# Graph attention and convolution on one core: products over 64 rows widened to 96 rows in the node stages

## The chip, the cores and the metric

The kernel runs on one core of one Trainium2 chip. The metric is the device time of one execution in microseconds (us). A core has TensorE (matrix products: weights are loaded, then columns are streamed through them), VectorE, ScalarE and GpSimd for element-wise work, and SyncE, which here only issues DMAs. The profile calls them PE (PEld for TensorE's weight loads), DVE, ACT, POOL and SP.

## The reference

6250 nodes with 160 features (64 scalars and 32 vectors of 3 components), 206250 edges sorted by their target. First a graph attention, then a graph convolution; both end in a residual and a layer norm over a node's features. What matters for the change are the products per node, cut from both layers:

```python
s_n, v_n = _equiv_layernorm(s, v, gamma_s, beta_s, gamma_v)      # per node
msg_s = (s_n @ Ws_src)[src] + (s_n @ Ws_dst)[dst]                # 64x64 each
msg_v = einsum('ncx,cd->ndx', v_n, Wv_src)[src] + einsum('ncx,cd->ndx', v_n, Wv_dst)[dst]
...                                                              # attention over edges
out = node + concatenate([agg_s @ Wps, einsum('ncx,cd->ndx', agg_v, Wpv)])
x = _layernorm(x + out)
# convolution
si_s, si_v = _irreps_linear(s_in, v_in, si_w0, si_w1)            # skip path, per node
h_s, h_v = _irreps_linear(s_in, v_in, lin1_w0, lin1_w1)          # gathered by the edges
...
x = _layernorm(x + s_skip + conv_out / 10.0)
```

## The kernel before, in words

The nodes lie in 49 blocks of 128 (nodes on partitions, features along the free dimension), the vectors with one component after the other, so that a block is 64 scalar columns and 96 vector columns. Everything is float32; a product appears in the trace as two passes (two weight loads and two MATMUL records), a transpose as one.

The kernel is a row of stages, each a block with its own instruction stream per engine and a barrier at its end:

1. attention_input: normalises the nodes and writes two tables, source and target, to memory.
2. attention_edges: gathers from them for 404 groups of 512 edges, computes logits and values.
3. segment_softmax, attention_aggregate: softmax over the edges of a node, sums into `agg`.
4. attention_output: divides by the softmax sum, projects (`wps`, `wpv`), adds to the nodes, layer norm, and projects again (`ts1`, `tv1`) into the table of the convolution and the skip path.
5. conv_edges, conv_output: the convolution over 452 steps, then the last products and the last layer norm.

The change lies in stages 1 and 4, from some 13 to 147 us and from 5236.5 to 5423 us of the span.

**attention_input.** Per block b, TensorE transposes the 64 scalar columns (L349) and the 96 vector columns (L350) into one bank of two; ScalarE moves them to SBUF with gamma and beta (L215, L217) into one buffer `feat` of four; TensorE multiplies: the 64 scalar rows with `ts0` (L356, 64 rows, 128 columns out) and the 96 vector rows with `tv0` (L358, 96 rows, 192 columns out) into one bank of four; VectorE copies the 320 columns to `out` (L337), and SyncE stores every half chunk. TensorE issues the transposes of block m ahead of the products of block m - 1. The nodes are normalised by VectorE in chunks of 3, 4 and six times 7 blocks (`EARLY0`); the eight steps of the next chunk's norm (L255 to L275) are spread between the copies of this chunk, and the last two steps (with L275 as the last) come after the copy of the last block but one. The transposes of a chunk wait for its last step. At b = 20 there is one more product (L362), over 64 rows. In the first 45 us GpSimd squares the edge vectors (L225 to L229) beside this.

**attention_output.** Two such pipelines run in one loop over m. The first ("u", block m): transposes L1132 and L1133, copy by ScalarE L1164 (96 partitions, 256 columns), products L1144 (`wps`, 64 rows, 64 columns out) and L1145 (`wpv`, 96 rows, 96 columns out), addition to the nodes by VectorE L1100. The second ("t", block m - 14, since its nodes must be normalised first, in chunks of 7): transposes L1138 and L1139, copy L1170, products L1152 (`ts1`, 64 rows, 128 columns out) and L1154 (`tv1`, 96 rows, 192 columns out), table copy by ScalarE L1178, skip addition by VectorE L1121. On TensorE the order in an iteration is L1132, L1133, L1138, L1139, L1144, L1145, L1152, L1154; the first 14 iterations have the u pair alone, the last 14 the t pair alone. All banks and feature buffers are double. VectorE also has the softmax division (L1057 to L1065, once per 7 blocks) and the norm (L1077 to L1092) in its stream.

In these transposes the scalars' one already takes 96 columns (`agg[:, b, 0:V3]`), of which the product reads 64 rows:

```python
pe.transpose(bt_u[b % 2][0:V3, 0:P], agg[:, b, 0:V3], w("ident"))
pe.matmul(bo_u[b % 2][:, 0:CS], feat_u[b % 2][0:CS, 0, :], w("wps"), start=True, stop=True)
```

`feat` is the stationary operand of each product (the profile's LDWEIGHTS, rows*columns "64*128" or "96*128"), the packed weights of `PACK` stream. `PACK` says for each weight how many rows it has; they all lie in one array of 128 partitions, filled on the host by `lay_pack`.

**conv_output** has products too (L1438, L1439, L1440), all over 128 rows, behind three transposes (L1432); it is not changed.

## Time and profile before

| | us |
|---|---|
| median of 3 runs (lowest to highest) | 7921.6 (7917.41 to 7922.39) |
| the profiled execution | 7914.6 |
| its span | 7912.8 |
| attention_input, to its last copy | 0 to 147.5 |
| attention_edges, softmax, aggregation | 147.5 to 5236 |
| attention_output, first transpose to last addition | 5236.6 to 5423.4 |
| conv_edges, conv_output | 5423 to 7912.8 |

The span is the time from the first to the last instruction of the profiled execution; its own time has what lies around that, 1.8 us. Starts in the rows below are us from the span's start. A row of the timeline has the start, the length, the engine, the line, the operation, what it writes and reads, the shape, and in brackets how long the engine had been idle and who released it; "x2" means that two records in a row were put together. The ends of MATMUL records are modelled, so distances between starts are safer than lengths. "issue" is idle time in which the engine waited for nothing that the profile shows. The clock is the one granted to TensorE as a share of 2.4 GHz.

### The profile page before, as it was taken

The page shows a single profiled execution, that of the slowest core. Times are in us where ns is not written, and L with a number is a line of the kernel's source. Part 1 is how long each engine was busy: PE and PEld are TensorE (multiplying, and loading weights), DVE is VectorE, ACT ScalarE, POOL GpSimd, SP SyncE. Part 2 cuts the span into 40 slices and gives each one's busy share as a digit, 9 for nine tenths or more (in the row PEclk, how much of TensorE's full clock was granted, in tenths as well). Part 3 has the DMA queues.
Part 4 walks back from the last instruction along what each step waited for, and adds up shares of the span by engine and source line. Part 5 has one row for each costly group of instructions (what it writes and reads, how often), then busy time and mean ns, then how long its engine had stood idle before and what let it go on. Part 6 is the DMA issues. An engine that isn't in the chain of part 4 may idle for free. (4 is left out here: it accounts for less than half of the span.)

```text
span 7912.8 us, 199441 instructions
## 1 busy us (share of the span) xinstructions
PE 7045.1 (89%) x48227; PEld 5905.9 (75%) x48227; DVE 7568.2 (96%) x18615; ACT 5259.2 (66%) x18286; POOL 5348.1 (68%) x5500
## 2 busy tenths in 40 slices
PE   6999999999999999999999859998888888888888
PEld 4888888888888888888888848875555555555556
DVE  4999999999999999999999889976999999999999
ACT  2666666666666666666666634435788788788786
POOL 2777777777777777777777436634777777777773
PEclk5999999999999999999999979977999999999999
DMA  3444444434434344343434337732333333333332
GB/s 105 107 109 109 106 107 106 107 106 106 107 105 107 106 107 106 106 108 105 107 106 107 89 128 260 257 117 69 94 93 91 90 91 90 91 91 90 91 91 59
DMA packets 815660, 856.41 MB, mean 108 GB/s; under 512 B 413920, under 2 KB 623200, under 8 KB 815072
## 3 DMA queue, kind: packets, MB, share of 16 engines
q0 software_dynamic: 241920, 413.20, 21.8%
q1 hardware_dynamic: 573088, 438.30, 18.1%
q10 hardware_dynamic: 576, 4.01, 0.1%
q8 instruction: 33, 0.54, 0.0%
q14 instruction: 43, 0.35, 0.0%
HBM read 706.51 MB, written 148.44 MB: 108 GB/s over the span
## 5 line engine op out<-in xcount | busy, mean ns | idle before, releaser
L1243 POOL DMA_INDIRECT agg<-tab_conv,ce_idx x1808 | 1708.7, 945 | 841.3 <-issue 621.8
L471 POOL DMA_INDIRECT ae_gdst<-tab_dst,ae_idx x1616 | 1683.9, 1042 | 528.0 <-issue 528.0
L468 POOL DMA_INDIRECT ae_gsrc<-tab_src,ae_idx x1616 | 1538.5, 952 | 674.4 <-issue 523.9
L1333 PE MATMUL psum<-ce_prod,ce_plain 128*128 128x384 f32 x3616 | 1539.7, 507 | 302.5 <-ACT ce_prod L1318 302.1
L1318 ACT ACTIVATE ce_prod<-ce_raw,ce_y 128x64 f32<-128x64 f32 x5424 | 1464.8, 333 | 0.0
L1316 ACT ACTIVATE ce_prod<-ce_raw,ce_y 128x160 f32<-128x160 f32 x1808 | 753.2, 417 | 488.8 <-DVE ce_raw L1264 488.8
L1335 PEld LDWEIGHTS psum<-ce_prod,ce_plain 128*128 128x128 f32 x3616 | 687.6, 190 | 479.6 <-issue 1.5
L713 ACT ACTIVATE ae_second_t<-psum 128x512 f32<-128x512 f32 x1212 | 732.2, 604 | 462.0 <-PE psum L623 456.1
L1333 PEld LDWEIGHTS psum<-ce_prod,ce_plain 128*128 128x128 f32 x3616 | 546.9, 191 | 449.5 <-DVE ce_plain L1294 276.2
L631 PE MATMUL psum<-pack_sb,ae_first_t 128*128 128x200 f32 x3232 | 850.1, 345 | 2.2 <-ACT ae_first_t L709 2.0
L641 PE MATMUL psum<-pack_sb,ae_second_t 128*128 128x96 f32 x3232 | 665.1, 288 | 129.1 <-ACT ae_second_t L713 126.7
L709 ACT ACTIVATE ae_first_t<-psum 128x512 f32<-128x512 f32 (+1 forms) x1212 | 692.0, 610 | 40.6 <-PE psum L614 40.6
L641 PEld LDWEIGHTS psum<-pack_sb,ae_second_t 128*128 128x128 f32 x3232 | 486.5, 190 | 241.6 <-issue 164.3
L614 PE MATMUL psum<-pack_sb,ae_first 128*128 128x128 f32 (+1 forms) x4848 | 662.9, 273 | 0.8 <-ACT ae_first_t L709 0.8
L719 ACT ACTIVATE ae_values<-psum 128x256 f32<-128x256 f32 x808 | 310.4, 384 | 523.8 <-PE psum L643 523.8
L1335 PE MATMUL psum<-ce_prod,ce_plain 128*128 128x96 f32 x3616 | 646.8, 261 | 0.0
L681 PE MATMUL psum<-pack_sb,ae_rbfy 64*128 64x224 f32 x3232 | 419.2, 374 | 255.0 <-DVE ae_first L540 231.1
L948 POOL TENSOR_TENSOR ag_exval<-ag_val,ag_wide 128x384 f32<-128x384 f32 x452 | 385.2, 852 | 380.9 <-ACT ag_exval L968 190.3
L643 PE MATMUL psum<-pack_sb,ae_second_t 128*128 128x96 f32 x3232 | 625.9, 275 | 0.0
L633 PE MATMUL psum<-pack_sb,ae_first_t 96*128 96x96 f32 x3232 | 625.8, 275 | 0.0
L642 PE MATMUL psum<-pack_sb,ae_second_t 128*128 128x96 f32 x3232 | 625.8, 275 | 0.0
L765 ACT ACTIVATE ae_second<-agg,ae_y_late 128x192 f32<-128x192 f32 x1616 | 598.2, 444 | 0.0
(216 smaller groups left out, 19066.1 us busy)
## 6 DMA issues: line engine op xcount, KB each, us to landing
ag_val<-h_dram SPq DMA_DIRECT2D x452, 320.0 KB, 4.0
h_dram<-ae_hout SPq DMA_DIRECT2D x404, 320.0 KB
agg<-in_query SPq DMA_DIRECT2D x452, 128.0 KB
ae_rin<-in_rin SPq DMA_DIRECT2D x404, 128.0 KB
agg<-tab_conv,ce_idx POOLq DMA_INDIRECT x1808
ae_gsrc<-tab_src,ae_idx POOLq DMA_INDIRECT x1616
ae_gdst<-tab_dst,ae_idx POOLq DMA_INDIRECT x1616
ce_idx<-in_eidx SPq DMA_DIRECT2D x452, 4.0 KB
```

What stands on the lines that cost most here:

```text
L468: pool.indirect_dma_start(gsrc[t.slot4][:, k, :], None, g["tab_src"], bass.IndirectOffsetOnAxis(ap=idx[t.slot4][:, k:k + 1], axis=0))\
L471: pool.indirect_dma_start(gdst[t.slot4][:, k, :], None, g["tab_dst"], bass.IndirectOffsetOnAxis(ap=idx[t.slot4][:, 4 + k:5 + k], axis=0))\
L614: ins = pe.transpose(b_t[b % 2][0:rows, P * k:P * k + P], first[t.slot][:, k, lo:lo + rows], w("ident"))
L631: pe.matmul(b_m[:, i, 0:200], first_t[0][:, e], w("m1_0"), start=True, stop=False)
L641: pe.matmul(b_h[:, i, 0:96], second_t[0][:, e], w("m2_0"), start=True, stop=False, skip_group_check=True)
L709: act.activation(first_t[b][0:rows, :], b_t[b % 2][0:rows, :], ACT.Copy).then_inc(kept, 1)
L713: act.activation(second_t[b][:, :], b_t[(b + 1) % 2][:, :], ACT.Copy).then_inc(kept2, 1)
L1243: pool.indirect_dma_start(node[t.slot8][:, k, :], None, g["tab_conv"], bass.IndirectOffsetOnAxis(ap=idx[t.slot8][:, k:k + 1], axis=0))\
L1316: act.activation(prod[t.slot][:, k, 0:160], raw[t.slot][:, k, 0:160], ACT.Identity, scale=y[t.slot8][:, k, 0:1])
L1318: ins = act.activation(prod[t.slot][:, k, 192 + 96 * x:256 + 96 * x], raw[t.slot][:, k, 160:WW], ACT.Identity, scale=y[t.slot8][:, k, x + ...
L1333: pe.matmul(b_a[t.slot], plain[t.slot4][:, k, :], prod[t.slot][:, k, 96:480], start=(k == 0), stop=False, skip_group_check=True)
L1335: ins = pe.matmul(b_a[t.slot][:, 96:384].rearrange("p (x c) -> p x c", x=3)[:, :, CS:96], plain[t.slot4][:, k, :], prod[t.slot][:, k, 0:96 ...
```

## The change

Three groups of products read 96 rows where they read 64. Their weights get 32 more rows, which are zero, so that the results stay. In attention_input the scalars' transpose takes 96 columns instead of 64 (the 32 more are the first vector columns), and ScalarE's copy 96 partitions, with gamma and beta zero in the added rows. The number and order of instructions, waits and DMAs are the same.

```diff
 PACK = [
-    ("ident", 128, 128), ("ts0", 64, 128), ("tv0", 96, 192), ("gamma_s", 64, 1), ("beta_s", 64, 1), ("gamma_v", 96, 1),
+    ("ident", 128, 128), ("ts0", 96, 128), ("tv0", 96, 192), ("gamma_s", 96, 1), ("beta_s", 96, 1), ("gamma_v", 96, 1),
...
-    ("k2_0", 128, 1), ("k2_1", 128, 1), ("k2_2", 128, 1), ("wps", 64, 64), ("wpv", 96, 96),
-    ("ts1", 64, 128), ("tv1", 96, 192), ("tp", 128, 224),
+    ("k2_0", 128, 1), ("k2_1", 128, 1), ("k2_2", 128, 1), ("wps", 96, 64), ("wpv", 96, 96),
+    ("ts1", 96, 128), ("tv1", 96, 192), ("tp", 128, 224),
...
-                        act.activation(feat[b % 4][0:CS, 0, :], b_t[b % 2][0:CS, 0:P], ACT.Identity,
+                        act.activation(feat[b % 4][0:V3, 0, :], b_t[b % 2][0:V3, 0:P], ACT.Identity,
                                        bias=w("beta_s"), scale=w("gamma_s"))
...
-                        pe.transpose(b_t[m % 2][0:CS, 0:P], normed[:, m, 0:CS], w("ident"))
+                        pe.transpose(b_t[m % 2][0:V3, 0:P], normed[:, m, 0:V3], w("ident"))
...
-                        pe.matmul(both[:, :, 0:CS], feat[b % 4][0:CS, 0, :], w("ts0").rearrange("p (o c) -> p o c", o=2),
+                        pe.matmul(both[:, :, 0:CS], feat[b % 4][0:V3, 0, :], w("ts0").rearrange("p (o c) -> p o c", o=2),
...
-                        pe.matmul(bo_u[b % 2][:, 0:CS], feat_u[b % 2][0:CS, 0, :], w("wps"), start=True, stop=True)
+                        pe.matmul(bo_u[b % 2][:, 0:CS], feat_u[b % 2][0:V3, 0, :], w("wps"), start=True, stop=True)
...
-                        pe.matmul(both[:, :, 0:CS], feat_t[b % 2][0:CS, 0, :], w("ts1").rearrange("p (o c) -> p o c", o=2),
+                        pe.matmul(both[:, :, 0:CS], feat_t[b % 2][0:V3, 0, :], w("ts1").rearrange("p (o c) -> p o c", o=2),
...
-    W["ts0"][:, :CS], W["ts0"][:, CS:] = L0["Ws_src"], L0["Ws_dst"]
-    W["ts1"][:, :CS], W["ts1"][:, CS:] = L1["lin1_w0"], L1["si_w0"]
+    W["ts0"][:CS, :CS], W["ts0"][:CS, CS:] = L0["Ws_src"], L0["Ws_dst"]
+    W["ts1"][:CS, :CS], W["ts1"][:CS, CS:] = L1["lin1_w0"], L1["si_w0"]
...
     for name in ("gamma_s", "beta_s"):
-        W[name][:, 0] = L0[name]
+        W[name][:CS, 0] = L0[name]
...
-    W["wps"][:] = L0["Wps"]
+    W["wps"][:CS] = L0["Wps"]
```

## Rows read from the trace of the kernel before

**Rows 1.** The page, part 1: busy us, share of the span, instructions.
```profile
PE 7045.1 (89%) x48227; PEld 5905.9 (75%) x48227; DVE 7568.2 (96%) x18615; ACT 5259.2 (66%) x18286; POOL 5348.1 (68%) x5500
```

**Rows 2.** Stretches: from:to, length, busy us (instructions) per engine, TensorE clock, DMA share, GB/s.
```profile
45.00:147.00 102.00, 91.16 (x258) 57.50 (x258) 50.37 (x122) 30.29 (x89) 0.00 (x0) 0.50 0.22 66
5236.50:5259.20 22.70, 22.12 (x82) 16.04 (x83) 14.21 (x34) 6.47 (x16) 13.64 (x1) 0.54 0.00 1
5262.00:5392.00 130.00, 130.00 (x411) 95.41 (x411) 58.79 (x131) 36.55 (x107) 0.00 (x0) 0.50 0.07 21
5392.00:5423.00 31.00, 30.53 (x87) 20.01 (x86) 11.46 (x24) 9.50 (x29) 0.00 (x0) 0.50 0.12 38
```

**Rows 3.** Waits, one of 45:147, one of 5262:5392: total us, times, longest.
```profile
PEld psum L356 <- issue: 15.5, 43, 0.4
...
DVE nodes L1100 <- PE psum L1145: 67.7, 30, 3.2
```

**Rows 4.** Timeline, attention_output, one block with both pairs: start, us, engine, line.
```profile
5264.73 0.42 PE L1132 MATMUL psum<-pack_sb,agg 128*96 128x128 f32 x1
...
5265.36 0.42 PE L1139 MATMUL psum<-pack_sb,nodes 128*96 128x128 f32 x1
...
5265.71 0.50 PEld L1144 LDWEIGHTS psum<-pack_sb,ao_feat_u 64*128 64x128 f32 x2 [0.36 <-issue]
...
5265.72 0.69 PE L1144 MATMUL psum<-pack_sb,ao_feat_u 64*128 64x64 f32 x2
...
5266.33 0.74 PE L1145 MATMUL psum<-pack_sb,ao_feat_u 96*128 96x96 f32 x2
...
5267.00 0.79 PE L1152 MATMUL psum<-pack_sb,ao_feat_t 64*128 64x128 f32 x2
...
5267.73 1.01 PE L1154 MATMUL psum<-pack_sb,ao_feat_t 96*128 96x192 f32 x2
...
5268.21 0.20 PEld L1132 LDWEIGHTS psum<-pack_sb,agg 128*96 128x96 f32 x1
...
5268.52 0.42 PE L1132 MATMUL psum<-pack_sb,agg 128*96 128x128 f32 x1
```

**Rows 5.** Timeline, conv_output, TensorE at the slower clock.
```profile
7853.16 0.85 PE L1432 MATMUL psum<-pack_sb,agg 128*128 128x128 f32 x3
...
7853.80 0.58 PE L1438 MATMUL psum<-pack_sb,co_feat 128*128 128x96 f32 x2
...
7854.55 0.64 PE L1440 MATMUL psum<-pack_sb,co_feat 128*128 128x64 f32 x2
...
7854.97 0.85 PE L1432 MATMUL psum<-pack_sb,agg 128*128 128x128 f32 x3
```

**Rows 6.** Stretches of the softmax stage and of conv_output, columns as in rows 2.
```profile
4631.00:4634.30 3.30, 2.99 (x13) 2.63 (x13) 0.00 (x0) 3.30 (x4) 0.00 (x0) 0.50 0.00 0
4634.50:4637.70 3.20, 0.63 (x4) 0.42 (x4) 0.00 (x0) 3.20 (x4) 0.00 (x0) 1.00 0.00 0
7853.20:7856.50 3.30, 3.30 (x18) 3.30 (x18) 1.95 (x4) 0.98 (x2) 0.00 (x0) 0.50 0.46 177
7856.60:7859.90 3.30, 3.30 (x33) 3.30 (x33) 3.27 (x6) 1.47 (x3) 0.00 (x0) 1.00 0.00 0
```

**Rows 7.** Timeline, attention_input, a chunk's first blocks and its end.
```profile
61.89 0.42 PE L349 MATMUL psum<-pack_sb,ai_normed 128*64 128x128 f32 x1 [2.16 <-DVE ai_normed L275]
...
63.98 0.42 PE L349 MATMUL psum<-pack_sb,ai_normed 128*64 128x128 f32 x1
...
76.75 0.49 DVE L337 COPY ai_out<-psum 128x320 f32<-128x320 f32 x1 [1.52 <-PE psum L358]
...
78.87 0.42 PE L349 MATMUL psum<-pack_sb,ai_normed 128*64 128x128 f32 x1 [2.16 <-DVE ai_normed L275]
```

**Rows 8.** Groups by line, 5262:5392: VectorE's additions of L1121, count, busy us, mean ns.
```profile
L1121 DVE TENSOR_TENSOR nodes<-nodes,psum 128x160 f32<-128x160 f32 x33 | 10.1, 306 | 0.0
```

**Rows 9.** Timeline, TensorE, the softmax stage's transposes before the clock rose.
```profile
4631.31 3.03 PE L832 MATMUL psum<-pack_sb,sm_logit 128*128 128x128 f32 x13 [23.45 <-ACT sm_logit L842]
```


## Prediction

> **What bounds the kernel now.** I read the page first [rows 1]: VectorE is busy for 96% of the span, so the two long edge stages are not TensorE's to shorten. But the change touches none of them: it lies in two short stages of node work, from 45 to 147 us and from 5236.5 to 5423 us. So the second view is a table of stretches [rows 2]. There the picture is the reverse: VectorE is busy 50 of 102 us in the first and 59 of 130 us in the middle of the second, while TensorE is busy nearly all the time, and its granted clock is 0.50, which is 1.2 GHz. The third view is who waits for whom [rows 3]: in the second stage VectorE waits 67.7 us for L1145, 30 times, and TensorE's weight loads stand idle for "issue" alone, as before L356, 43 times up to 0.4 us. So TensorE's own sequence sets the pace here, and every 0.1 us taken from it per block comes off the end, as the stages follow one another behind barriers.
>
> Fourth comes the timeline of one block of attention_output [rows 4]. The four transposes before L1144 stand 0.21 us apart (5264.73 to 5265.36 in the row of L1132 and L1139, three steps). Then comes a hole: L1144, over 64 rows, starts 0.36 us after L1139, and its weight load starts with it, not ahead of it. From L1144 to L1145 0.61, to L1152 0.67, to L1154 0.73, to the next L1132 0.79 us. The last step has no hole: the weights of L1132 (128 rows) are loaded from 5268.21, 0.31 us ahead of its start, while L1154 (96 rows) still runs. So from 96 to 128 rows TensorE prefetches, and at each step between 64 rows and 96 or 128 it doesn't. The block repeats every 3.80 us.
>
> **The change, part by part.** It changes three groups of 49 products (L356, L1144, L1152) from 64 rows to 96. It adds no instruction, DMA, wait or buffer; the order on all queues stays.
>
> What a product costs without the hole is seen in conv_output, where all have 128 rows and where the clock was for a while also 0.50 [rows 5, 6]. There the three transposes take 0.64 us (0.213 each) with the first product right behind them, two products of 96 and 64 columns take 0.75 us together, and the third 0.42, so 0.37 to 0.42 each. A product of 128 columns streams twice what a transpose of 128 does, 2 x 0.213 = 0.43. One of 192 columns is 1.5 times that, 0.64; that is also the 0.79 of L1154 less the first weight load of some 0.15 that would be prefetched. I take 0.40, 0.40, 0.43 and 0.64.
>
> At 1.2 GHz:
> - attention_input: a block takes 2.09 us inside a chunk (61.89 to 63.98) [rows 7]. New: 0.43 of transposes + 0.43 + 0.64 = 1.49, so 0.60 less. At the chunk's end the last products also come 0.60 earlier, and the wait behind them (eviction, normalisation, 76.75 to 78.87) keeps its length. 42 blocks and the last product: 43 x 0.60 = 25.8 us. The blocks before 45 us count nothing: there VectorE stands still beside GpSimd's squares, whose start a DMA sets.
> - attention_output, first 14 blocks, transposes and L1144/L1145 alone (22.7 us): 0.43 + 0.40 + 0.40 = 1.23 us for the first seven, 8.6 us. In the next seven VectorE is late instead: its work for seven blocks is 12.0 us (58.79 us over 34.2 blocks), less seven additions of 0.306 us [rows 8] which come later, 9.9, with some waits 11. Sum 19.6, so 3 us less.
> - 35 blocks with both pairs: 4 x 0.213 + 0.40 + 0.40 + 0.43 + 0.64 = 2.72 instead of 3.80: 35 x 1.08 = 37.8 us. VectorE needs 1.72 us of the 2.72, so it stays hidden.
> - 14 last blocks with L1152/L1154 alone, a pattern as in attention_input: 14 x 0.60 = 8.4 us.
>
> Together 75 us. What is priced at nothing: the transpose L349 with 96 instead of 64 columns (a load of 96 columns takes 0.20 us [rows 4], so it grows by at most a third of that, 0.07, while the last pass of L358 still streams for half of 0.64); the activation L215 over 96 partitions instead of 64 (128 elements per partition either way; ScalarE is busy 30 of 102 us); the scaling of ts1 over 96 rows, as many elements per partition as now. If that cover is gone, the load costs 49 x 0.07 = 3.4 us. The product L362 keeps its 64 rows and its holes, once.
>
> **The clock.** This is where I had to choose. In the two stages the clock stays at 0.50 (1.2 GHz) all the time, but for the first us of the second [rows 2]. At conv_output it was 0.50 too, and after 3.3 us of products and transposes back to back it rose to 1.00 (2.4 GHz) [rows 6]; and so it did in the softmax stage after 3 us of 13 transposes back to back [rows 6, 9]. What the node stages lack against these is the unbroken stream: it is cut at each change of rows, four times in 3.80 us. After the change a chunk of attention_input is one stream of 7 x 1.49 = 10.4 us, and the middle of attention_output one of 95 us. So I expect TensorE to reach 2.4 GHz in most of both stages, and VectorE to set the pace then:
> - attention_input: VectorE's work per chunk is 50.37 / 6 = 8.4 us, with about 1.1 us (half of 2.09) for a chunk's first block, through which VectorE waits, 9.5. Each chunk would begin at 1.2 GHz after the idle stretch at the border, so I take halfway between 9.5 and the 12.8 (17.0 - 7 x 0.60) of the slow clock: 11. Six chunks: 6 x (17.0 - 11) = 36 us.
> - attention_output with both pairs: 1.72 us of VectorE per block plus what it can't use in light slots, 2.1 us: 35 x 1.7 = 59.5, less 4 for stretches at the low clock, 55. Last 14 blocks: 31 us [rows 2] become 18, the normalisation of the last chunk and then about 1 us per block: 13. First 14: 3 as above.
>
> Sum 107 us; as the clock will fall back at some places that I can't see, I take **100 us**. Between no gain of the clock (75) and VectorE's bound at all times (some 120) lies the range of this case.
>
> **The base.** The profiled execution took 7914.6 us (span 7912.8), 7.0 us less than the median of the runs, 7921.6. Against its own time the forecast is 7814.6; against the median 7821.6. A difference under 0.2% (16 us) can't be told from none here.
>
> **Rivals.**
> - *The holes go, the clock stays at 1.2 GHz.* For it: the padded products fill 96 of the array's 128 rows, where the work before both rises [rows 5, 9] filled all 128, and no row shows a clock that rose over products of 96. Against it: no row tells one kind of work from the other either, and the stages that stayed slow had holes. The gain is the sum of the four parts above, 75: 7846.6 us.
> - *The holes go, but transposes don't bring the full clock*, and the stream of both stages is a third transposes (0.85 of 2.72 us, 0.43 of 1.49), cutting it up as the holes did. Against it: after 13 transposes alone [rows 9] the clock rose from 0.50 to 1.00 [rows 6]. The same 75 us: 7846.6 us. This one is a rule of the Trainium skill (TensorE: Matmul & The Clock Gate, Part 4: PE-mode transpose): the full clock does not engage for transpose mode. As far as the softmax rows go, the trace disagrees.
> - *The change doesn't do what it says*: the hole belongs to the hand-over from a transpose to a product, or to reading what ScalarE has just written, not to the rows. Against it: conv_output has the same hand-over with no hole [rows 5], and L1152 stands between two products and has one. Time as now, 7921.6 us.
> - *Slower:* the holes stay for that reason, and each padded product pays for 96 rows. The nearest price is the step after L1145 (96 rows, 96 columns; 0.67) against the one after L1144 (64, 64; 0.61): 0.06 x 147 = 9 us, 7930 us. It would be measurable as slower from 0.11 us per product (16 / 147).
>
> **How the numbers follow.** The full clock for most of both stages: 0.60, at 7822, own range 7802 to 7838. Low clock throughout: 0.22 by the filling and 0.05 by the transposes, at 7847, give or take 6. One stage at one clock and one at the other gives 7810 to 7845, within these; 0.06. The range 7800 to 7852 takes in all of these. Holes stay: 0.05. Slower mechanism: 0.02. Faster: 0.60 + 0.22 + 0.05 + 0.06 = 0.93; same 0.05; slower 0.02.
>
> **What would show it.** In the profile after: no "issue" idle at L356, L358, L1144, L1152 and L1154, and weight loads there that start ahead of the products; the block of attention_output with both pairs 2.7 us at a clock of 0.50 or near 2.1 at 1.00; a granted clock of 1.00 in most of attention_output; VectorE's waits for L358 and L1145 down to a fraction. The edge stages and conv_output must keep their lengths. I am wrong if the holes are still there, if the clock stays at 0.50 (then some 25 us too low), or if the block is longer than 2.7 us because a wait between VectorE and TensorE (two accumulator buffers, L1100 and L1121) takes the place of the holes.

## The result, and the profile after

The changed kernel took 7796.63 us (median of 6 runs, 7793.98 to 7802.3), the kernel before 7917.93 us in the same comparison (6 runs, 7913.09 to 7922.39): ratio 0.9848, 95% interval 0.9836 to 0.9861. The gain is 121 us where 100 were forecast, and the time lies 3 us below the range. The profiled execution took 7797.69 us, 116.9 us less than the one before.

How the lengths of the stages moved, each taken from the starts of its instructions in the two traces. "u", "both" and "t" are the parts of attention_output: the blocks with L1144/L1145 alone, with both pairs, and with L1152/L1154 alone.

| us | before | after | difference | forecast |
|---|---|---|---|---|
| attention_input, first L349 to last L337 | 133.5 | 89.9 | -43.6 | -36 |
| edge stages to the first L1132 | 5089.6 | 5092.0 | +2.4 | 0 |
| attention_output, u | 22.6 | 21.9 | -0.7 | -3 |
| attention_output, both | 130.9 | 69.2 | -61.7 | -55 |
| attention_output, t | 33.0 | 17.3 | -15.7 | -13 |
| conv_edges | 2414.4 | 2415.1 | +0.7 | 0 |
| conv_output | 72.1 | 74.4 | +2.3 | 0 |

The +2.4 and +2.3 are no effect: the unchanged kernel after, profiled again, had 5089.0 and 72.3. The differences add up to -116.3 us, and the first transpose starts 0.6 us earlier; that is the 116.9 us between the two profiled executions.

Part 1 of the page after [rows 1]:

```profile
PE 6907.1 (89%) x48227; PEld 5838.2 (75%) x48227; DVE 7567.1 (97%) x18615; ACT 5254.6 (67%) x18286; POOL 5365.6 (69%) x5500
```

As many instructions as before. The shares say nothing about this change. The stretches do [rows 2]:

```profile
43.00:54.00 11.00, 8.94 (x42) 7.80 (x42) 8.51 (x20) 5.07 (x15) 0.00 (x0) 0.70 0.29 88
54.00:63.70 9.70, 6.40 (x42) 5.14 (x42) 8.58 (x20) 5.07 (x15) 0.00 (x0) 0.98 0.39 120
5194.70:5216.70 22.00, 17.37 (x82) 14.86 (x82) 16.81 (x34) 6.48 (x16) 13.67 (x1) 0.55 0.00 1
5216.70:5286.00 69.30, 58.59 (x416) 53.56 (x416) 58.35 (x133) 31.60 (x108) 0.00 (x0) 0.95 0.13 39
5286.00:5303.50 17.50, 13.60 (x93) 11.22 (x91) 11.55 (x25) 9.29 (x31) 0.00 (x0) 1.00 0.22 67
```

The granted clock, 0.50 in all of this before but for the first 2 us of attention_output, is 0.95 over the blocks with both pairs and 1.00 over the last. The first two rows are a chunk of attention_input at a mean clock of 0.70 and the next at 0.98; the same 42 records (transposes and products) keep TensorE busy for 8.94 and 6.40 us.

One block of attention_input while the clock was still 0.50 [rows 7]:

```profile
44.70 0.42 PE L349 MATMUL psum<-pack_sb,ai_normed 128*96 128x128 f32 x1
44.91 0.42 PE L350 MATMUL psum<-pack_sb,ai_normed 128*96 128x128 f32 x1
44.91 0.55 PEld L356 LDWEIGHTS psum<-pack_sb,ai_feat 96*128 96x128 f32 x2
45.13 0.63 PE L356 MATMUL psum<-pack_sb,ai_feat 96*128 96x128 f32 x2
45.55 0.85 PE L358 MATMUL psum<-pack_sb,ai_feat 96*128 96x192 f32 x2
46.19 0.42 PE L349 MATMUL psum<-pack_sb,ai_normed 128*96 128x128 f32 x1
```

L356's weight load now starts 0.22 us ahead of the product, beside the transpose L350. The block takes 1.49 us (44.70 to 46.19), as the forecast had it (0.43 + 0.43 + 0.64); it was 2.09.

A block of attention_output with both pairs at full clock [rows 4], and the waits of that stretch, 5224 to 5286 us [rows 3] (us in total, times, longest):

```profile
5250.56 0.46 PE L1152 MATMUL psum<-pack_sb,ao_feat_t 96*128 96x128 f32 x2
...
5251.19 0.27 PE L1132 MATMUL psum<-pack_sb,agg 128*96 128x128 f32 x1
...
5251.52 0.27 PE L1139 MATMUL psum<-pack_sb,nodes 128*96 128x128 f32 x1
5251.63 0.33 PE L1144 MATMUL psum<-pack_sb,ao_feat_u 96*128 96x64 f32 x2
5251.80 0.41 PE L1145 MATMUL psum<-pack_sb,ao_feat_u 96*128 96x96 f32 x2
5252.48 0.46 PE L1152 MATMUL psum<-pack_sb,ao_feat_t 96*128 96x128 f32 x2 [0.27 <-DVE nodes L1121]
```

```profile
PEld psum L1152 <- ACT ao_feat_t L1170: 10.4, 13, 1.0
PE psum L1152 <- DVE nodes L1121: 10.3, 18, 0.9
DVE nodes L1100 <- PE psum L1145: 6.3, 6, 1.3
```

L1144 follows the transpose L1139 by 0.11 us, the same step as between transposes. VectorE's wait for L1145, 67.7 us before, is 6.3; in its place TensorE waits ahead of L1152 for VectorE's L1121, 18 times. The block that took 3.80 us takes 1.44 to 2.55 once the clock has risen, and seven of them 13.67.

One row was not foreseen. GpSimd zeroes agg1 (the tile agg in the row) beside the u part:

```profile
5192.59 15.78 POOL L1049 MEMSET agg<- 128x18816 f32 x1 [2.62 <-POOLq L928]
5205.14 3.26 DVE L1079 TENSOR_SCALAR ao_mean<-ao_mean 128x7 f32<-128x7 f32 x1
5208.57 0.66 PE L1144 MATMUL psum<-pack_sb,ao_feat_u 96*128 96x64 f32 x2 [2.29 <-DVE nodes L1100]
```

L1079 takes 0.17 us in its other chunks. Here it took 3.26 and ended with the memset (5208.37); L1100 stood behind it, and TensorE, idle for 2.29 us, behind that. In the kernel before, L1079 began as the memset ended, because the u part was slower.

### The profile page after: what moved, and what is told of

The parts are those of the page before. It is cut to its first block and busy times, and to the rows that moved or that the text cites. A ratio compares the mean times of both kernels' runs of the same rounds, so it can differ in the third digit from the quotient of the medians.

```text
span 7795.9 us, 199441 instructions
## 1 busy us (share of the span) xinstructions
PE 6907.1 (89%) x48227; PEld 5838.2 (75%) x48227; DVE 7567.1 (97%) x18615; ACT 5254.6 (67%) x18286; POOL 5365.6 (69%) x5500
## 5 line engine op out<-in xcount | busy, mean ns | idle before, releaser
L681 PE MATMUL psum<-pack_sb,ae_rbfy 64*128 64x224 f32 x3232 | 419.2, 374 | 256.9 <-DVE ae_first L540 229.9
L633 PE MATMUL psum<-pack_sb,ae_first_t 96*128 96x96 f32 x3232 | 625.9, 275 | 0.0
```

## The experiments

The theory: a change of contracted rows costs TensorE a hole, and the cut stream of products keeps its clock at 1.2 GHz; padding removes both, and then VectorE sets the pace. The rivals: the hole belongs to something else; the clock rose for another reason; the time came from elsewhere. A hole is the time lost where a product's weights are loaded with it and not ahead of it.

Of these runs only e9 to e12 ran on a chip like the first; on the others' chips the edge stages took 3.6 to 4.0 ms longer for every kernel, so runs are compared by the lengths of the node stages, which there agree with the first profiles. On those chips the median of a whole kernel is known to some 0.3 to 0.9% only, more than most of these changes are worth.

| us, profiled run | attention_input | u | both | t | conv_output |
|---|---|---|---|---|---|
| e1_input_only | 89.9 | 23.0 | 130.9 | 33.0 | 73.0 |
| e2_output_only | 133.5 | 21.9 | 69.2 | 17.3 | 72.5 |
| e3_t_only | 132.3 | 22.7 | 112.6 | 18.8 | 73.9 |
| e4_regroup | 132.5 | 22.7 | 119.3 | 33.5 | 70.5 |
| e5_conv_holes | 89.8 | 21.9 | 72.2 | 17.3 | 74.7 |
| e6_conv_edges_128 | 90.0 | 21.9 | 72.2 | 17.3 | 75.1 |
| e7_memset_pieces | 92.0 | 19.3 | 69.8 | 18.9 | 72.8 |
| e8_squares_pieces | 81.5 | 21.9 | 69.1 | 17.3 | 72.2 |
| e9_late_holes | 90.1 | 21.9 | 82.2 | 18.8 | 71.3 |
| e10_pieces | 79.7 | 19.9 | 68.4 | 18.9 | 72.7 |
| e11_squares_act | 81.3 | 24.7 | 69.1 | 20.7 | 76.2 |
| e12_after | 89.8 | 21.9 | 69.0 | 17.3 | 72.3 |
| e13_spread | 80.1 | 19.1 | 67.5 | 20.0 | 75.0 |
| e14_spread_squares | 81.8 | 20.3 | 65.4 | 20.6 | 73.3 |
| e15_pieces_again | 79.5 | 19.9 | 68.4 | 18.9 | 75.1 |
| e16_add_first | 81.0 | 19.6 | 78.2 | 18.7 | 72.1 |
| e17_add_first_all | 84.2 | 20.3 | 60.1 | 17.2 | 73.2 |
| e18_after_again | 89.8 | 21.9 | 72.3 | 17.8 | 74.4 |

How far a stage varies by itself is seen where its code is the same: conv_output, which only e5 changes, took 70.5 to 76.2 us, and attention_input of e8, e10, e11 and e13 to e17 79.5 to 84.2. Each run was profiled once.

**Each stage alone.** The change was split, on the kernel before: L356 with what feeds it (e1), and L1144 and L1152 (e2). The edits here and below are cut to the words that change.

```
e1:  - feat[b % 4][0:CS, 0, :], w("ts0")    + feat[b % 4][0:V3, 0, :], w("ts0")
e2:  - feat_u[b % 2][0:CS, 0, :], w("wps")  + feat_u[b % 2][0:V3, 0, :], w("wps")
     - feat_t[b % 2][0:CS, 0, :], w("ts1")  + feat_t[b % 2][0:V3, 0, :], w("ts1")
```

> The change in attention_input alone. Theory (the two stages are independent, each gains by its own holes and its own clock): the gain of attention_input in the changed kernel, 44 us (last copy of L337 at 102.8 instead of 147.0), comes whole, so 7918 - 44 = 7874 us, attention_output keeps its 186.5 us and a clock of 0.50. Rival (the work of one stage brings something to the other): the two parts run alone don't add up to 121 us; less than 30 or more than 60 us here.

> The change in attention_output alone. Theory: 78 us less (186.5 becomes 108.5), 7840 us, with a clock of 1.00 over most of the stage; attention_input keeps 147 us at 0.50. Rival, as for the run with attention_input alone: far from 78, so that both don't add up.

Each stage took its new length and the other kept its old one. Ratios 0.9923 (0.9883 to 0.9963) and 0.9947 (0.991 to 0.9985). The two parts of the change add up, and neither acts on the other's stage. Of the edge stages these two runs tell nothing: up to the first L1132 they took 8106.7 and 8179.1 us.

**Which step makes the hole.** e3 pads L1152 only. e4 pads nothing and puts the 64-row products next to each other, so that a block changes between 64 rows and 96 or 128 twice instead of four times.

```
e3:  - feat_t[b % 2][0:CS, 0, :], w("ts1")   + feat_t[b % 2][0:V3, 0, :], w("ts1")
e4:  order  - L1144 L1145 L1152 L1154        + L1144 L1152 L1145 L1154
```

> Only L1152 (ts1) gets 96 rows; L1144 and L356 keep 64. Theory (a hole at each change of rows, and the clock stays at 0.50 as long as the stream is cut): the block with both pairs goes from 3.80 to 3.24 us (0.64 for transposes, 0.36 and 0.61 around L1144 as before, 0.56 for L1145 with its first load still open, 0.43, 0.64), at 0.50; in the last 14 blocks no hole is left, so the clock rises there and they take about 17 us instead of 33. Gain 20 + 16 = 36 us, 7882 us. Rival (what counts for the clock is how much is streamed, not that it is unbroken): 0.50 becomes 1.00 with both pairs too, block near 2.1 us, gain about 70 us, 7848 us.

> No product is padded. In attention_output the order of products is L1144, L1152 (64 rows), then L1145, L1154 (96 rows), so that a block with both pairs changes rows twice after the transposes instead of four times; the rest is the kernel before. Theory (the hole belongs to the change of rows): 3.80 becomes 3.3 us (0.64, 0.36, 0.55, 0.57, 0.55, 0.64) at a clock of 0.50; 35 blocks, gain 17 us, 7901 us, and no hole between L1144 and L1152 nor between L1145 and L1154. Rival (a hole stands before every product over 64 rows, whatever ran before it): the hole before L1152 stays, the block stays over 3.6 us, gain under 7 us.

e3: 3.26 us a block at clock 0.50, where 3.24 was expected; t 18.8 instead of 33.0; ratio 0.9963 (0.9933 to 0.9992). e4: blocks of 3.37 to 3.72 us at clock 0.50, 24.3 for seven, and 11.6 us gained over the stretch; in between what was expected (3.3 and 17) and the rival's bounds (3.6 and 7). For e4 there is no ratio; its runs took 11575.6 to 11866.1 us. Its rows, weight loads (PEld) and products (PE; L1146 is the L1144 of before, L1150 the L1152, L1153 the L1145):

```profile
8328.27 0.50 PEld L1146 LDWEIGHTS psum<-pack_sb,ao_feat_u 64*128 64x128 f32 x2 [0.36 <-issue]
8328.73 0.50 PEld L1150 LDWEIGHTS psum<-pack_sb,ao_feat_t 64*128 64x128 f32 x2
8329.45 0.50 PEld L1153 LDWEIGHTS psum<-pack_sb,ao_feat_u 96*128 96x128 f32 x2 [0.22 <-issue]
8329.83 0.55 PEld L1156 LDWEIGHTS psum<-pack_sb,ao_feat_t 96*128 96x128 f32 x2
```

```profile
8328.27 0.69 PE L1146 MATMUL psum<-pack_sb,ao_feat_u 64*128 64x64 f32 x2
8328.76 0.77 PE L1150 MATMUL psum<-pack_sb,ao_feat_t 64*128 64x128 f32 x2
8329.46 0.74 PE L1153 MATMUL psum<-pack_sb,ao_feat_u 96*128 96x96 f32 x2
8329.99 0.90 PE L1156 MATMUL psum<-pack_sb,ao_feat_t 96*128 96x192 f32 x2
```

The loads of L1146 and L1153, after a change from 128 to 64 and from 64 to 96, start with their product and not ahead of it. The load of L1150 comes 0.03 us ahead of its product, 0.46 us after the last: between 64 and 64 rows the large hole is gone, but the load is still not taken early. L1156 (96 after 96) is loaded 0.16 us ahead. So the hole belongs to the change of rows, and 64-row products keep a smaller one of their own; the rival that it belongs to the hand-over from the transpose falls with e1 to e3. The Trainium skill (TensorEngine Tiling (Array Packing), Tiling Modes: Available Configurations and Key Properties) says that changing the tiling mode drains TensorE, and lists 64 rows as a mode and none between 64 and 128: the trace agrees, 96 and 128 rows following each other without a hole, but no row names the mode of a product.

**Holes where the clock is already high.** The theory would have conv_output lose its clock if a product there had 64 rows (e5, which leaves out the other half of that product). In e9 L1144 has 64 rows again from block 28 on.

```
e5:  - feat[b % 4][:, 1, :], w("l2b")     + feat[b % 4][0:64, 1, :], w("l2b")[0:64, :]
e9:  + r = V3 if b < 28 else CS
     - feat_u[b % 2][0:V3, 0, :], w("wps")   + feat_u[b % 2][0:r, 0, :], w("wps")[0:r]
```

> The changed kernel with holes put where none were: in conv_output the product L1439 reads 64 of its 128 rows (the other half of that product is left out). Theory: the load of each L1439 comes 0.35 us after the pass before it at the lower clock, the next product's as well, and the cut stream brings conv_output, which ran at a mean clock of 0.83 to 0.87 and about 74 us, down to 0.50; a block of 1.81 us at that clock becomes about 2.3, 49 blocks some 110 us, so 30 to 40 us longer. Rival (VectorE sets the pace of conv_output anyway, and the clock does not mind short holes): 74 us, give or take 4.

> The kernel after, with L1144 over 64 rows again from block 28 on, that is from the middle of attention_output's stretch with both products, when the granted clock has been 1.00 for about 20 blocks; every product is computed as before, only two changes of rows a block return. The run with a 64-row product in conv_output kept its clock at 1.00 in spite of its holes, against the theory that holes hold the clock down. Theory A (a hole only keeps a clock from rising; one that has risen stays): a block goes from 1.9 us to about 2.0 to 2.2 with clock 1.00, and the stretch with both products ends 0 to 6 us later (69.2 -> 70 to 75). Theory B (with these shorter products, holes bring the clock back to 1.2 GHz): within some blocks the clock falls to 0.50 and a block takes 3.3 us as in the run with only the later product padded, so the last 21 blocks cost some 28 us more (69.2 -> 90 to 100).

e5 was a miss. The granted clock stayed at 1.00 through the stage, and its length was 74.7 us:

```profile
11430.00:11444.00 14.00, 13.54 (x97) 11.72 (x98) 5.78 (x13) 5.29 (x11) 0.00 (x0) 1.00 0.01 2
11444.00:11497.00 53.00, 49.67 (x345) 42.02 (x343) 47.50 (x85) 18.58 (x44) 0.00 (x0) 1.00 0.14 55
```

```profile
11460.38 0.50 PE L1432 MATMUL psum<-pack_sb,agg 128*128 128x128 f32 x3
11460.72 0.36 PE L1438 MATMUL psum<-pack_sb,co_feat 128*128 128x96 f32 x2
11461.01 0.43 PE L1439 MATMUL psum<-pack_sb,co_feat 64*128 64x64 f32 x2
11461.37 0.43 PE L1440 MATMUL psum<-pack_sb,co_feat 128*128 128x64 f32 x2
11461.64 0.50 PE L1432 MATMUL psum<-pack_sb,agg 128*128 128x128 f32 x3
```

The holes are there: a block takes 1.26 us (11460.38 to 11461.64) against 0.95 in the kernel after, and 0.15 us for each of two changes is half the slow clock's hole (0.60 us for two in attention_input). VectorE, busy 47.50 of 53 us, hides them. It is without the holes that this stage loses the full clock, as in the kernel after:

```profile
7718.00:7792.00 74.00, 57.12 (x441) 55.29 (x441) 60.17 (x111) 24.08 (x56) 0.00 (x0) 0.83 0.12 50
```

There TensorE runs ahead of VectorE, and every seven blocks or so one takes 1.96 to 3.92 us with the wait in it; after those of 3.92, 3.55, 3.01 and 2.80 us the next took 1.81 us, a block at clock 0.50, after that of 1.96 not. In e5 the faster pace is gone, and so is the long wait: the longest block takes 2.08 us. In the stage of every other profile the clock fell at least twice, in e5 not once. That the shorter waits are the cause is not shown: after waits as long the clock has stayed up too (a block of 3.30 us in the kernel before).

e9 shows the other side, in attention_output from block 28 on. Its stretches from where the holes begin (5247.6) to the fall, and after it:

```profile
5246.50:5272.50 26.00, 23.43 (x152) 18.94 (x150) 22.34 (x53) 11.64 (x41) 0.00 (x0) 1.00 0.13 39
5272.50:5299.50 27.00, 27.00 (x100) 22.04 (x101) 12.49 (x26) 8.50 (x25) 0.00 (x0) 0.50 0.09 28
```

For 25 us nothing is to be seen but somewhat longer blocks; then the clock falls to 0.50 for 37.5 us, and each block with both pairs takes 3.26 us, as in e3. Theory B holds in kind (its 90 to 100 us for the stretch were too much, as the fall came late: 82.2). So in this stage one 64-row product a block, with its two changes, is enough to keep the clock down (e3, over all of its 112.6 us) and, in the one profile of e9, to bring it down; in conv_output it is not. No run parts the holes from the 64 rows themselves, since both come and go together, and what makes the two stages differ was not settled.

**Holes elsewhere in the kernel.** L1345 in the long conv_edges stage contracts 64 rows as well, among products of 128. In the kernel before, that stage was granted the full clock (1.00 from 6000 to 7800 us) with these products in it, eight records of 64 rows in a step of some 5.3 us, and so was attention_edges (1.00 from 1000 to 2000 us) with L681 over 64 rows and L633 over 96.

```
e6:  - query[t.slot8][q:q + CS, e:e + P], w("tp")[q:q + CS, :]
     + query[t.slot8][:, e:e + P], w("wy")[:, q:q + WW]
     with w("wy") = w("tp") in two halves, the other 64 rows of each zero
```

> The same idea in conv_edges, on top of the change: the four 64-row products of a step (L1345) read all 128 rows, with weights that are zero in one half. Theory (worth something only where TensorE sets the pace): per step TensorE waits 0.65 us for ScalarE before L1333; the padded products take eight passes of 0.187 us one after the other, 1.5 us instead of 1.03, less two holes of about 0.15; the 0.3 us more goes into that wait, so conv_edges keeps its length within 1% (2415 us where the edge stages run as in the first profiles). Rival 1 (a hole is a hole anywhere): 0.3 us less per step, 452 steps, 130 us less. Rival 2 (the 64-row products overlapped in pairs and that is lost on the path): 0.3 us more per step or above, 130 to 200 us more.

conv_edges took 3251.4 us beside 3232.0, 3253.6 and 3236.5 in e5, e7 and e8 of the same chip. No gain, no loss, as expected. But this is a chip on which the stage takes a third longer than in the first profiles, with VectorE busy for 2258 of 3000 us: TensorE does not set the pace there, and what the same edit would do where VectorE is busy all the time (first profiles) was not run.

**GpSimd in VectorE's way.** The memset of the row above, and the three operations on squares in attention_input, cut into pieces.

```
e7:  - pool.memset(g["agg1"][:, :, :], 0.0)
     + for a in range(BLOCKS): ins = pool.memset(g["agg1"][:, a, :], 0.0)
e8:  L225, L227 and L229 in a loop over 16 pieces each
e10: both
```

> The changed kernel, with GpSimd's memset of agg1 (15.8 us in one instruction) in 49 pieces. Theory (the 3.26 us of L1079 in the first blocks of attention_output are VectorE standing still until the memset ends): L1079 takes 0.17 us, the part with the first pair alone goes from 21.9 to about 18.8 us, 3 us less; the rest stays. Rival (the wait is a semaphore or the table load of ScalarE beside it): no difference.

> The changed kernel, with each of GpSimd's three operations on the edge vectors in attention_input (8.7, 3.0 and 4.4 us) in 16 pieces. Theory (the same standing still: VectorE's L258, L262, L263, L269 end when GpSimd's instruction ends): the seven blocks up to 43 us lose most of their 15 us of such waits, first transpose to the seventh block 30.2 us to about 19, so 11 us less. Rival (VectorE waits for GpSimd's whole work or for the data of the DMA): no difference.

> The kernel after with the memset of agg1 in 49 pieces and the three GpSimd operations on the squares in 16 pieces each. Separately these took 2.6 us off attention_output's first stretch (21.9 -> 19.3) and 10.9 us off the time to attention_input's seventh block (30.2 -> 19.3), of which 8.3 stayed at the end of that stage. If the two are independent: attention_input 89.9 -> 81.5, u part 19.3, together 11 to 13 us less than the kernel after run beside it. Rival: what VectorE gains early is given back by a clock that rises at another time; then less than 5 us stays in one of the two stages.

> The kernel with the pieces again, beside the two that build on it, so that they can be compared on one chip: attention_input about 80 us, attention_output 107, ratio to the kernel before 0.984.

VectorE in attention_input, first the kernel after, then e8 (L262 is L270 there, L263 is L271, L269 is L277), and GpSimd beside it in the kernel after:

```profile
25.47 8.10 DVE L262 TENSOR_TENSOR ai_normed<-nodes,ai_mean 128x448 f32<-128x448 f32 x1
33.50 2.92 DVE L263 TENSOR_SCALAR ai_var<-ai_var 128x7 f32<-128x7 f32 x1
38.04 2.88 DVE L269 TENSOR_SCALAR ai_var<-ai_var 128x7 f32<-128x7 f32 x1
```

```profile
25.79 0.80 DVE L270 TENSOR_TENSOR ai_normed<-nodes,ai_mean 128x448 f32<-128x448 f32 x1
26.51 0.66 DVE L271 TENSOR_SCALAR ai_var<-ai_var 128x7 f32<-128x7 f32 x1
29.23 0.26 DVE L277 TENSOR_SCALAR ai_var<-ai_var 128x7 f32<-128x7 f32 x1
```

```profile
24.83 8.27 POOL L225 TENSOR_TENSOR ai_ysq<-ai_yraw 128x4848 f32<-128x4848 f32 x1 [24.40 <-DMA ai_yraw<-in_yall]
33.17 3.21 POOL L227 TENSOR_TENSOR ai_ysum<-ai_ysq 128x1616 f32<-128x1616 f32 x1
36.46 4.43 POOL L229 TENSOR_TENSOR yy<-ai_ysum,ai_ysq 128x1616 f32<-128x1616 f32 x1
```

Each of VectorE's long rows ends about where GpSimd's operation does (33.6 and 33.1, 36.4 and 36.4, 40.9 and 40.9). In pieces, each waits for one piece only. Block 7, counted from 0, comes 19.3 us after the first instead of 30.2, as expected; at the stage's end 8.3 us remain. In e7 the memset's pieces take 0.42 us each and L1079 0.41 at the first chunk; u is 2.6 us shorter, but t 1.6 longer, since the clock there was lower (0.82 against 1.00). The Trainium skill (SBUF — State Buffer, Who interferes with whom) says that VectorE and GpSimd share a port pair, that VectorE takes it in its two-port modes, or with two inputs in SBUF beside a GpSimd instruction that reads SBUF, and that the one that comes second is then blocked for the whole of the other's instruction. The rows agree: L262, with two inputs, was held beside L225, which reads; beside the memset, which only writes, L1062 with two inputs kept its 0.62 us (from 5199.12), and only L1079 was held, with L1100 behind it. That L1079 runs in a two-port mode no row shows.

e10, on the chip like the first, took 7788.2 us (7781.6 to 7790.9), ratio 0.9837 (0.9821 to 0.9853); beside it e12, the kernel after unchanged, took 7798.7 us (7792.6 to 7799.5), ratio 0.9849 (0.9833 to 0.9866). The four runs of each don't overlap. In the stages touched 11.2 us are gained (10.1, 2.0 and 0.7, less 1.6), as expected if the two are independent; but 10.1 for 8.3 in attention_input is within what that stage varies by.

> The kernel after unchanged, on the same chip and in the same rounds as the runs beside it, so that they can be compared with it as well as with the kernel before. Stage lengths as in its first profile: attention_input 89.9, attention_output 108 to 111 us. On a chip whose edge stages take 11,400 us the whole should come out 121 us under the kernel before, a ratio of about 0.99.

e15, the same as e10 on the other chip, had e10's stage lengths to 0.2 us, conv_output apart.

**What bounds the blocks with both pairs.** Four steps on top of e10: e11 gives ScalarE the squares of the norm; e13 spreads the rescaling of agg; e14 does both; then L1121 is put first, in e16 on e10 and in e17 on e14.

```
e11: - norm(c, 3) on VectorE (L1083)
     + act.activation(square[:, 0:4, :], nodes[:, a:a + 4, :], ACT.Square)   at m % 7 == 2
     + act.activation(square[:, 4:7, :], nodes[:, a + 4:a + 7, :], ACT.Square)   at m % 7 == 3
e13: - if at == 3: share(m // 7 + 1)
     + if at in (4, 6): half of share(m // 7 + 2)   and share(1) at m == 1
e16: dve.tensor_tensor(nodes[:, b, :], ..., bo_t[b % 2][:, C:2 * C], ALU.add)   ahead of norm(c, ...)
```

> The run before it, and the squares of the norm in attention_output (L1083, 1.32 us on VectorE once in seven blocks) made by ScalarE in two halves. Theory (VectorE is what now bounds the stretch with both products: 53.5 of 62 us busy, PE 51.3): 1.3 us come off each of some five groups of seven blocks, 69.2 -> 62 to 65 us, and little in the part with t alone. Rival (TensorE waits for ScalarE's copies, which stand behind the halves of 0.7 us): the stretch stays at 69 us or over.

> The run with the pieces, and VectorE's rescaling of agg in attention_output (share: L1057 to L1065, 2.1 us once in seven blocks), which fell in the same block as the norm's 1.5 us, made one group of seven earlier and halved between two blocks of the group that have little of the norm. Theory C (what bounds the stretch with both products is the blocks in which VectorE's work is bunched, not its sum): the seven blocks go from 13.7 us to 12.3 to 12.9, the stretch from 68.4 to 62 to 65 us. Rival D (VectorE's sum bounds it): nothing changes, 68 to 69 us. Rival E (the chain of waits from TensorE to ScalarE and back does): nothing changes either, and the 1.15 us wait of VectorE for L1145 stays in each group.

> The same with the squares of the norm on ScalarE in two halves, which alone moved nothing (13.67 -> 13.70 us for seven blocks). Theory C: now that no block holds more of VectorE's work than two of the norm's 1.3 us operations, the 1.3 us come off as well: 11.2 to 12 us for seven blocks, the stretch 57 to 61 us. Rival E: ScalarE's copies behind the squares hold TensorE up, and it stays where the run beside it is.

> The run with the pieces, and VectorE's addition L1121 put before the norm's operation of the same block instead of behind it. TensorE's L1152 of the next block waits for this addition, and the sum it takes from PSUM has been there since the block before. Theory F (what bounds the stretch with both products is TensorE waiting for an addition that stands behind a 1.3 us operation): the wait of L1152 for L1121 goes, and the seven blocks come from 13.7 us to between VectorE's own 11.9 (53.5 of 62 us busy) and 12.6, the stretch from 68.4 to 60 to 64 us. Rival D (VectorE's sum and its queue): 67 to 69 us, the wait turning up before L1145 or in ScalarE.

> The same reordering on the kernel with the rescaling spread and the squares on ScalarE (13.06 us for seven blocks). Theory F: nothing of VectorE's then stands before TensorE, and the seven blocks come near seven times the shortest block of all these runs, 1.44 us: 10.1 to 11 us, the stretch 51 to 57 us. Rival E (ScalarE's copies behind its squares): it stays over 60 us, with TensorE waiting for L1170's copy.

e11 (whole kernel 7792.3 us, ratio 0.984, 0.9824 to 0.9856): 13.7 us for seven blocks, as in e10. Taking 1.3 us from VectorE moved a wait and nothing else, so its sum isn't the bound. Its u part, 24.7 us for 19.9, has a cause of its own: here VectorE's small operation (L1079 before, L1089 in e11) did not get in between the pieces of the memset, but waited until the last had ended, at 5201.0:

```profile
5196.66 4.37 DVE L1089 TENSOR_SCALAR ao_mean<-ao_mean 128x7 f32<-128x7 f32 x1
```

```profile
5196.26 4.75 POOL L1058 MEMSET agg<- 128x384 f32 x13
```

In the profiles of the seven other runs with these pieces it took 0.20 to 0.41 us. So the pieces open gaps, but do not ensure that VectorE gets one. e13: 13.06 us, 0.6 less, so bunching is a part of it, but the smaller part; theory C's 12.3 to 12.9 was a miss. e14: 13.06 again, a miss for theory C (11.2 to 12). Ratios 0.9884 (0.9841 to 0.9927), 0.9879 (0.9814 to 0.9943), and 0.9889 (0.9809 to 0.9969) for e15 beside them: no difference.

e16 is the telling miss (78.2 us, for 60 to 64 by theory F and 67 to 69 by rival D). Where nothing delays them its blocks take 1.44 us, five in a row or so; at the bunched block TensorE then waits more than before, the block takes 3.9 to 4.3 us, and the clock falls. Its stretches:

```profile
8155.20:8168.90 13.70, 11.64 (x92) 10.73 (x91) 12.07 (x30) 6.72 (x24) 0.00 (x0) 1.00 0.14 43
8168.90:8175.70 6.80, 6.80 (x31) 6.37 (x30) 3.90 (x9) 2.42 (x7) 0.00 (x0) 0.50 0.12 36
8175.70:8182.50 6.80, 5.27 (x43) 4.74 (x41) 6.28 (x16) 3.42 (x12) 0.00 (x0) 1.00 0.03 10
8182.50:8192.80 10.30, 10.06 (x43) 9.51 (x44) 5.78 (x14) 3.48 (x10) 0.00 (x0) 0.50 0.17 51
```

43 records take 6.8 us in one row and 10.3 in the next. The stretch came to 78.2 us, 10 more than e10's, although the wait that was to go was down to the bunched blocks (3.9 us, 3 times, for 10.3 us, 18 times in the kernel after). The whole kernel points the same way: 11506.2 us, ratio 0.998 (0.9941 to 1.0019), against 11450.6 for e18 beside it, whose interval it just touches.

```profile
PE psum L1162 <- DVE nodes L1115: 3.9, 3, 1.4
```

(L1162 there is L1152, L1115 is L1121.) e17 has no bunched block, and there the same step pays:

```profile
8116.00:8169.90 53.90, 49.03 (x382) 44.55 (x380) 45.05 (x113) 32.44 (x111) 0.00 (x0) 1.00 0.17 50
```

The clock holds, seven blocks take 12.1 us, the stretch 60.1. That is 8 us less than e10 but over theory F's 57; TensorE's load for L1144 (L1161 there) now waits for ScalarE's copy, so theory F and rival E each have a part:

```profile
PEld psum L1161 <- ACT ao_feat_u L1189: 6.7, 9, 1.2
```

Over attention_input and attention_output e17 takes 181.8 us against 201.8 of e18, the kernel after on the same chip (198.1 in e12). That sum of stages is what is known of e17: its whole time, 11459.7 us, and e18's, 11450.6, can't be told apart on that chip (ratios 0.989, 0.9847 to 0.9933, and 0.9918, 0.9888 to 0.9947).

> The kernel after unchanged beside the two, as the run to compare them with on this chip: attention_input 89.8, attention_output 108 us.

In e18 the clock rose 3.4 us later and fell once for 6.8 us in the middle of the stretch with both pairs, which took 72.3 us instead of 69.2; so it did in e5 and e6. In the kernel after, e2, e8 and e12, with the same code there, it did not.

## Why the prediction was right, and where not

**The holes** were right, and so were their sizes: 1.49 us for a block of attention_input, 1.23 in the u part (both measured in the trace after), 2.77 for a block with both pairs while the clock was low, for 2.72. "The edge stages and conv_output must keep their lengths": right within what they vary by (+2.4, +0.7 and +2.3 us).

**The clock** was the choice that decided, and it went the way that had been given 0.60. The rival that transposes would hold it down fell: four of the eight operations of a block are transposes, and the granted clock is 1.00. The rule behind it, the Trainium skill's (TensorE: Matmul & The Clock Gate, Part 4: PE-mode transpose), is answered by the softmax rows [rows 6, 9], where 13 transposes alone stand before the rise, more than by this, since here the products may have brought the clock up by themselves. That padding the 64-row products is what lets the clock rise is shown for attention_output by e3 and e9. The reason given for it, an unbroken stream, is not, so the choice was right in part by luck: after the change TensorE still waits 18 times ahead of L1152, up to 0.9 us, at a clock of 1.00, and the edge stages and e5 have full clock with 64-row products in the stream. The trace of the kernel before had the edge stages' rows, and the prediction did not look at them.

**What failed is the size of the terms at full clock**, all in one direction. The step "I take halfway between 9.5 and the 12.8 [...] of the slow clock: 11" for a chunk of attention_input: the chunks took 11.1, 9.4, 11.5, 10.0 and 10.0 us, mean 10.4, at mean clocks of 0.70, 0.98, 0.72, 0.83 and 0.83; and the last part of the stage, priced like the others, ran at 1.00 and shrank from 16.5 to 7.6 us. Together -43.6 for -36. The step "2.1 us: 35 x 1.7 = 59.5, less 4 for stretches at the low clock": a block took 13.67 / 7 = 1.95, and -61.7 was measured for -55. The t part gave 15.7 for 13 (2 of that because it is counted from 5390 here and from 5392 there). Last, the step "as the clock will fall back at some places that I can't see, I take 100 us" of a sum of 107 put another 7 us on the wrong side: it did not fall back between 5224 and 5303, and where it did (e5, e6, e18) the stretch was 3.1 us longer. These come to 7.6 + 6.7 + 2.7 + 7 = 24 us. In the other direction, the u part gave 0.7 for 3 through the memset, which the rows of before had hidden, since VectorE came to L1079 just as it ended. The differences of the edge stages and of conv_output, +5.4 in the two profiles, are what such stages vary by. With the start 0.6 earlier that leaves the 116.9 us of the profiled executions; the medians of the six runs differ by another 4.4, in all 121.3.

The lower end of the range, 7800, stood for "VectorE's bound at all times (some 120)". It was no bound: it was added up with 2.1 us a block and 18 us for the t part, which took 1.95 and 17.3. And 3.7 us of the miss are the base: the kernel before had 7921.6 us in its first three runs and 7917.93 in the six of the comparison. Against the first base the same gain would have come out at 7800.3, inside the range, so whether the time fell within it was chance; that 100 was too low by a fifth was not.

What keeps the block above VectorE's 1.72 us had been put down to "light slots" of VectorE. The runs show a chain instead: L1152 waits for an addition that stands behind a 1.3 us operation, and a bunched block adds to that; VectorE's sum is not it (e11). Putting the addition first paid only once nothing was bunched (e17 against e16).

## What to carry to other kernels

Among products of 96 or 128 contracted rows one of 64 costs two holes in TensorE's sequence, some 0.3 us each at the slow clock and 0.15 at the full one (e5); if it has partitions to spare, pad it with zero weights, provided TensorE sets the pace there (where it doesn't, e6 gained nothing and lost nothing). Look then for the second effect, a clock that can rise, and read it in the profile after: here the holes were worth some 75 us by the forecast's block lengths, which the trace bore out, and the clock the other 46 or so (an estimate). And once it has risen, even out the other engines' work before shortening any of it: removing a wait but leaving a bunch cost 10 us (e16), removing both gave 8 (e17).

## What the runs showed that was not expected

- A 64-row product's weight load is not taken early even behind another of 64 rows (0.03 us ahead instead of 0.16, e4).
- Holes of the same kind left conv_output at full clock for 67 us (e5), where without them the clock fell at least twice in every profile; in attention_output it fell 25 us after they began (e9).
- A GpSimd memset, which reads nothing, held a VectorE operation on 7 numbers a partition for 3.26 us; 8.3 us of squares held one of 0.8 us for 8.1. Once a row of 13 short memsets did the same (e11). Cutting the memset and the squares into pieces took 10.5 us off the median (7798.7 to 7788.2).
